# A Mamba block with expert feed-forward on one core: another order for ScalarE, TensorE and VectorE within a chunk, and another home for the convolution's sums

## The reference, cut to what matters

```
h    = x @ W.T + b + 2 * (x @ A[adapter]) @ B[adapter]             # cond, per batch adapter
u, g = split(h @ W_in.T)                                           # 2048 channels each
u    = silu(conv4(u) + conv_b)                                     # causal, 4 taps per channel
dt, Bm, Cm = rmsnorm of the parts of u @ Wx.T                      # 64 + 16 + 16
delta = softplus(dt @ Wdt.T + dt_bias)
state[t] = exp(delta[t] * A) * state[t-1] + (delta[t] * u[t]) * Bm[t]   # 16 states per channel
y[t] = sum over the 16 states of state[t] * Cm[t];  y = (y + u * D) * silu(g)
x2   = x + y @ W_out.T
z    = x2 @ base_W + base_b + lora(x2);  8 experts of rank 64, the 2 best by softmax gate
out  = x2 + sum over experts of weight * (z @ A_e.T) @ B_e.T
```

## Time and profile before

| | |
|---|---|
| median of 3 timed runs | 2613.73 us (2610.88 to 2616.55) |
| profiled execution | 2611.66 us, span 2609.9 us |
| busy: PE, DVE, POOL, ACT | 2321.2, 2239.9, 2121.8, 1622.4 us |
| granted TensorE clock, mean | 0.95 |
| first scan, end of last scan | 135.7 us, 2546.5 us |

### The profile page before, as it was taken

The page is one execution under the profiler, slowest core; times in us unless marked ns, Lnnn a source line. Parts: engine busy times, 40 slices in busy tenths (PEclk is TensorE's granted clock), DMA queues, the critical chain, the costliest instruction groups (busy, mean ns, idle before and its releaser), DMA issues.

```text
span 2609.9 us, 30425 instructions
## 1 busy us (share of the span) xinstructions
PE 2321.2 (89%) x10128; PEld 1911.7 (73%) x10128; DVE 2239.9 (86%) x2084; ACT 1622.4 (62%) x3751; POOL 2121.8 (81%) x1092
## 2 busy tenths in 40 slices
PE   8977998799989999899989999899988987786968
PEld 6866675488777878688777878688777866665857
DVE  1277777589999999999999999999999999999892
ACT  1466555466667766776667766776667766775550
POOL 0087776689889998999889998999889998999770
PEclk9988998899999999899999999899999999888989
DMA  6352433434346434543336434544336333522322
GB/s 213 125 199 85 113 105 111 129 124 137 113 127 199 140 128 131 182 145 137 113 127 199 141 128 131 182 145 137 112 107 202 126 108 101 170 92 97 121 84 97
DMA packets 131511, 350.04 MB, mean 134 GB/s; under 512 B 38609, under 2 KB 43217, under 8 KB 129883
## 3 DMA queue, kind: packets, MB, share of 16 engines
q1 hardware_dynamic: 108600, 296.18, 35.1%
q10 hardware_dynamic: 22756, 51.92, 6.0%
HBM read 337.03 MB, written 11.02 MB: 133 GB/s over the span
## 4 chain that ended last, share of the span: by engine, by line
PE 55%; POOL 14%; DVE 13%; ACT 9%; issue 7%; DMA 1%; ACTq 0%; SPq 0%; POOLq 0%; DVEq 0%
PE ubank L573 9%; PE gbank L594 8%; PE late L639 8%; DVE scan L1196 7%; POOL st L1396 6%; POOL st L1404 6%; ACT scan L1038 4%; PE gbank L603 4%; PE small L555 3%; PE late L674 3%; DVE st L1208 3%; PE late L555 3%; PE scan L573 2%; PE small L755 2%; PE late L613 2%
## 5 line engine op out<-in xcount | busy, mean ns | idle before, releaser
L1196 DVE TENSOR_TENSOR_SCAN scan<-scan,st 128x1024 f32<-128x1024 f32 x512 | 1153.4, 2285 | 192.5 <-ACT scan L1038 171.8
L1396 POOL TENSOR_TENSOR st<-w_sb,bc 128x1024 f32<-128x1024 f32 x512 | 1196.9, 2358 | 77.7 <-PE gbank L603 49.8
L1038 ACT ACTIVATE scan<-delta,A_sb 128x255 f32<-128x255 f32 x2048 | 846.5, 459 | 0.0
L1404 POOL TENSOR_TENSOR st<-st 128x1024 f32<-128x1024 f32 x256 | 603.0, 2356 | 214.9 <-DVE st L1208 204.9
L594 PE MATMUL gbank<-h,wt 128*128 128x256 f32 x2048 | 488.3, 394 | 20.1 <-DVE yg L1222 19.4
L594 PEld LDWEIGHTS gbank<-h,wt 128*128 128x128 f32 x2048 | 402.7, 198 | 93.2 <-DVE yg L1222 27.1
L1208 DVE TENSOR_TENSOR st<-scan,bc 128x1024 f32<-128x1024 f32 x384 | 455.2, 1213 | 0.0
L573 PE MATMUL ubank<-h,wt 128*128 128x256 f32 x1712 | 419.2, 401 | 0.0
L639 PE MATMUL late<-yg,wt 128*128 128x256 f32 x1792 | 401.2, 382 | 0.0
L1035 ACT ACTIVATE scan<-iota 128x4 f32<-128x4 f32 x512 | 86.6, 169 | 501.3 <-DVE st L1208 455.9
L573 PEld LDWEIGHTS ubank<-h,wt 128*128 128x128 f32 x1712 | 348.1, 204 | 58.2 <-issue 3.6
(11 more groups left out here) (193 smaller groups left out, 2445.7 us busy)
## 6 DMA issues: line engine op xcount, KB each, us to landing
wt<-in_W_in SPq DMA_DIRECT2D x256, 512.0 KB, 3.7
wt<-in_W_out SPq DMA_DIRECT2D x128, 512.0 KB, 3.3
wt<-in_cond_W SPq DMA_DIRECT2D x64, 512.0 KB, 3.6
bc<-bc_rows ACTq DMA_DIRECT2D x64, 512.0 KB, 6.5
wt<-G_tiles SPq DMA_DIRECT2D x32, 512.0 KB, 3.7
wt<-in_ffn_B SPq DMA_DIRECT2D x32, 512.0 KB, 3.4
xb<-in_x SPq DMA_DIRECT2D x8, 1024.0 KB, 6.2
x<-in_x ACTq DMA_DIRECT2D x28, 256.0 KB, 3.6
```

What stands on the lines that cost most here:

```text
L1038: last = fn(t[:, k, 1:T], delta[:, c, 1:T], ACT.Exp, scale=A_sb[:, col:col + 1])
L1196: v_.tensor_tensor_scan(Tps[q % 2][:, :], Tps[q % 2][:, :], x_, 0.0, ALU.mult, ALU.add).then_inc(scan_done, 1)
L1396: tt(st[:, n % ST_RING, :, :], w_sb[:, i % 2:i % 2 + 1, :].to_broadcast([P, NQ, T]), bc[:, 0, q * NQ:(q + 1) * NQ, :], ALU.mult).then_inc( ...
L1404: tt(st[:, n % ST_RING, :, :], st[:, n % ST_RING, :, :], st[:, (n - 1) % ST_RING, :, :], ALU.add).then_inc(add_done, 1)
```

## The change

ScalarE: decay 2 comes first in the slot (behind the evacuations), then the u evacuation of the chunk that TensorE made in the slot before, the evacuation of the half job, decay 3, silu of the gate, silu of u, the table load, and decay 0 and 1 of the next chunk. Softplus moves up to the slot's start.

TensorE: the gate chunk goes to the right half of `ubank`, the u chunk stays in the left half. Jobs get three lanes: late (bank `late`), small (bank `small`) and half (right half of `gbank`), dealt out anew over the slots, with single-block jobs `Bs`; xp and the first dt job become an end job behind the gate chunk. The order is late, small, state sum, half, u, gate, end job, and the parts of the last batch's W_out. u and gate wait for silu of the gate and for the u evacuation.

VectorE: y_sum and y_gate come behind the last product; y_sum also waits for the half job. The taps come between `add_first` and scan 2, one slot later. They add up in a new SBUF tile `cv`, into which ScalarE writes the fourth tap; only the 16 chunks of the prologue keep PSUM. The softmax's second half is spread over one slot in six steps.

G: gate and expert columns lie together (`GT_all`), and each of the 8 steps is a matmul with 264 and one with 256 columns instead of one with 8 and one with 512. The bias row is made in four column groups of TensorE and stored as four rows.

```diff
 def u_evac(v):
-    fn(o[:, T:2 * T], o[:, 0:T], ACT.Identity, bias=cb[:, c:c + 1], scale=cw[:, c, TAPS - 1:TAPS]).then_inc(u_ev, 1)
+    fn(cv_home(v), o[:, 0:T], ACT.Identity, bias=cb[:, c:c + 1], scale=cw[:, c, TAPS - 1:TAPS]).then_inc(u_ev, 1)
+def cv_home(v):
+    return quarter(v % 4)[:, T:2 * T] if v < NC else cv[:, v % 2, :]
 def conv_tap(v, k):
-    cv = u_home(v)[:, T:2 * T]
-    v_.scalar_tensor_tensor(cv, up[:, e, k:k + T], cw[:, c, k:k + 1], cv, ALU.mult, ALU.add)
+    v_.scalar_tensor_tensor(cv_home(v), up[:, e, k:k + T], cw[:, c, k:k + 1], cv_home(v), ALU.mult, ALU.add)
@@ TensorE, a slot
-    sum_states(i - 1); run(first_job(i), i); u_chunk(us[0]); out_part; run(late_job(i), i)
-    u_chunk(us[1]); run(last_job(i), i); gate_chunk(i + 1)
+    run(late_job(i), i); run(small_job(i), i); sum_states(i - 1); run(half_job(i), i)
+    ubank_free(i)                        # q_done(i + 1), u_ev of the slot before
+    u_chunk(v) for v in us; gate_chunk(i + 1); run(end_job(i), i); out_part
@@ ScalarE, a slot
-    evac(late, last of i - 1); u_silu(i - 1); wait gate_mm; silu of gate; exp table
-    decay(i, 2); decay(i, 3); evac dt, wT; u_evac(i); softplus; decay(i + 1, 0); decay(i + 1, 1)
+    evac(late, small, end of i - 1); softplus; decay(i, 2); wait gate_mm; u_evac(i - 1); evac(half of i - 1)
+    decay(i, 3); silu of gate; u_silu(i - 1); exp table; decay(i + 1, 0); decay(i + 1, 1)
@@ VectorE, a slot
-    scan 0; evac; scan 1; evac; mul 0; mul 1; add_first; scan 2; scan 3; y_sum; y_gate; mul 2; mul 3; taps(i)
+    scan 0; evac; scan 1; evac; mul 0; mul 1; add_first; taps(i - 1); scan 2; scan 3; mul 2; mul 3; y_sum; y_gate
@@ a g job
-    mm(gbank[:, T + k * E:T + (k + 1) * E], wt[kk], GTg[:, kk, :]); mm(o[:, :], wt[kk], GTx(kk))
+    mm(o1, wt[kk], GTx(kk)[:, 0:GX]); mm(o2, wt[kk], GTx(kk)[:, GX:])      # GX = 264
...
```

More of the change, by code:

```diff
@@ L163, in job_tiles @@
         return [("B", b, k)]
+    if kind == "Bs":
+        return [("Bs", b, k)]
     if kind == "g":
@@ L173, in slot_tiles @@
     tiles = []
-    us = u_chunks(i)
-    if first_job(i):
-        tiles += job_tiles(first_job(i))
+    for job in (late_job(i), small_job(i), half_job(i)):
+        if job:
+            tiles += job_tiles(job)
     if i == 0:
         tiles += [("cond", 1, m) for m in range(4, KH)]
-    if us:
-        tiles += [("u", us[0], 0)]
+    tiles += [("u", v, 0) for v in u_chunks(i)]
+    if i + 1 < CHUNKS:
+        tiles += [("gate", i + 1, 0)]
+    if end_job(i):
+        tiles += job_tiles(end_job(i))
     if part_job(i):
@@ L440, in softplus_of @@
         def softplus_of(i):
[L442 to L448, removed]
+            return [job[1:] for job in slot_jobs(i - 1) if job[0] == "dt"] if i >= 1 else []
         @block.sync
@@ L675, in expert_in, with expert_one, transformed @@
                 return mm(o, b2g[:, m * P:(m + 1) * P], la2[:, :], start=False, stop=True)
+            def expert_one(f, m, o):
+                n = TILE_NO[("Bs", f, m)]
+                pe.wait_ge(*loaded(n))
+                for k in range(EK):
+                    last = mm(o, wt[:, n % W_RING, k, :], hw[:, k, :], start=(k == 0), stop=(k == EK - 1))
+                return last
+            def transformed(rows, o1, o2):
+                for kk in range(KH):
+                    mm(o1, rows(kk), GTx(kk)[:, 0:GX], start=(kk == 0), stop=(kk == KH - 1))
+                    last = mm(o2, rows(kk), GTx(kk)[:, GX:], start=(kk == 0), stop=(kk == KH - 1))
+                return last
             def weights_t(o):
@@ L757, in run @@
+                    transformed(lambda kk: wt[:, n % W_RING, kk, :], o[:, 0:GX],
+                                late[:, 0:T] if k < KH - 1 else gbank[:, T:2 * T]).then_inc(inc, 1)
                 elif kind == "b2":
                     pe.wait_ge(b2_ld, 16 * B)
-                    rows = [b2_all[:, kk, :, :].rearrange("p b r -> p (b r)") for kk in range(KH)]
+                    pe.wait_ge(yg_done, i - 1)
+                    transformed(lambda kk: b2_all[:, kk, :, :].rearrange("p b r -> p (b r)"), o[:, 0:GX],
+                                gbank[:, T:2 * T]).then_inc(inc, 1)
+                else:
+                    pe.wait_ge(yg_done, i - 1)
@@ L771, in run @@
+                        last = mm(gbank[g:g + 1, T:2 * T], base_bias[:, kk:kk + 1], GTx(kk)[:, GX:],
+                                  start=(kk < GR), stop=(kk >= GR))
                     last.then_inc(inc, 1)
@@ L1330, in _ @@
                 mul(i, 1)
+                if weigh:
+                    soft_max_step(b - 1, 3)
                 add_first(i)
-                if b and c == 9:
-                    soft_max_in(b - 1)
+                if weigh:
+                    soft_max_step(b - 1, 4)
+                if i:
+                    for v in u_chunks(i - 1):
+                        for k in range(TAPS - 1):
+                            conv_tap(v, k)
+                if weigh:
+                    soft_max_step(b - 1, 5)
@@ L1365, in _ @@
             soft_max_in(LAST)
-            soft_max_out(LAST)
+            for n in range(6):
+                soft_max_step(LAST, n)
             for m in range(EK):
```

566 lines of the change are left out of this document (293 added, 273 removed).

## The result

The changed kernel took 2802.57 us (median of four runs, 2801.43 to 2807.97) against 2613.16 for the kernel before on the same chip: 1.073 times the time, 95% interval 1.0709 to 1.0746. It is 7% slower. The forecast was 2914 with a range of 2570 to 3010, from case A, in which the taps wait for GpSimd. The profiled run took 2807.97.

A forecast was written before the change was run, and what follows sets the result against it. No single bound at first (VectorE's own work about 279 us a batch); with waiting taps VectorE bounds. Batches 2 to 5 +220, 1 +39, 6 +51, 7 -8, 0 even: 2611.7 + 302 = 2914 us, range 2570 to 3010.

The forecast's parts named there:

- case A: Taps with two SBUF inputs each wait for the running GpSimd instruction; 2914 us, own range 2740 to 3010, chance 0.57.
- the CAST's rows: VectorE CAST with operands in SBUF: median 1.67 us, seven of eight waited for GpSimd; taken as nearest evidence for taps.
- the taps' wait per batch: VectorE's three taps a slot waiting for GpSimd, summed over the slots: 66 us a batch.
- its gain of 50: Batch 0, stage by stage, comes to 309 us without tap waits, a gain of 50; tap waits eat it.
- The 3.6 of y sum: y_sum, waiting for the half job, stalls about 1.2 us in each of slots 6 to 8, 3.6 a batch.
- the 7 of x_proj: x_proj behind u and gate in slot 12 stalls slot 13 by 4 to 6 us; with late silu 7 a batch.
- Case C: Taps don't wait; the state sum freed from silu decides, mainly in batch 0: 2539 us, chance 0.24.
- Case B: Only the first of three taps waits, 15.6 us a batch: 2609 us, about no change, chance 0.19.
- The 0.2 lost at the first tap: First tap can start at 8.45 but VectorE is there at 8.25: 0.2 us lost a slot, 3 a batch.
- decay first: ScalarE's decay 2 ahead of the u evacuation: could gain nothing in a 17.1 us slot.
- Y behind the last product: y sum and y gate moved to cover decay 0: 0.7 to 0.8 us a slot gained, in batch 7 only.
- The short products: 16 short TensorE instructions go from each of eight g jobs, 1.75 us each; only batch 0 sees it.

The follow-up runs named there:

- experiment 1: Changed kernel, but taps from chunk 16 on read u in PSUM, so they have one SBUF input; 2532.00 us, 0.969 of the kernel before.
- experiment 4: Changed kernel, but only the first of three taps has two SBUF inputs, its sum going to PSUM; 2622.80 us, 1.003 of the kernel before.
- experiment 5: 15 of x_proj's 16 products moved ahead of TensorE's silu wait in slot 12: on experiment 1's kernel 2505.29 us, on the changed kernel 2801.88 us.
- experiment 6: On experiment 1's kernel: y sum and y gate back ahead of the last two products, 2627.89 us; separately, decay 2 back behind the evacuations, 2520.31 us.
- experiment 7: Experiment 1's kernel with 16 short products of 8 columns again in each g job and the b2 job; 2566.20 us, 0.982 of the kernel before.
- experiment 2: Kernel before, with only the convolution sum cv moved from PSUM to SBUF from chunk 16 on; 2949.04 us, 1.129 of the kernel before.

## Why the prediction was right, and what it mis-sized

- **Right in sign and mechanism: case A.** The taps wait for the GpSimd instruction that runs, and the two take turns, as said. What makes them wait is the second SBUF input (experiments 1 and 4), as in the rule that the prediction cites; its other ground, the CAST's rows, was luck, as the last section shows. The mean, 1447 ns, is just under the 1.5 to 2.5 forecast.
- **The term that was too large is the taps' wait per batch.** I had 66 us; batch 2 has 50.8, batch 1 50.8, batches 3 to 5 46.7 to 49.5, batch 0 39.7 (50 as 37 + 13), batch 6 36.2 (51). The rest of the sum held: 278.9 + 3.8 + 50.8 = 333.5, and batch 2 took 333.8 (forecast 348.7). Batch 0 took 344.8, where its gain of 50 was to be eaten whole, batch 1 334.8 for 351. Of the 111 us between forecast and result 14 lie in batch 0, 16 in batch 1, 15 to 19 in each of batches 2 to 5, and 14 in batch 6. By slot of batch 2 I was too high above all where I let a tap meet a GpSimd product that in truth still waited for the state sum: slot 1 (4.3, measured 1.7) and 8 (2.5, 1.0), where neither the second nor the third tap waits, and 9 (5.9, 3.0) and 14 (6, 2.7), where the second doesn't. The state sum ends at 10 to 14 us of those slots, behind the late and small jobs, and not at 5 to 8.7. Slots 0, 3, 12 and 15 came within 1 (5.6, 4.3, 5.9, 6.1). Over the whole kernel 80 of the 112 first taps wait, 72 of the second and 55 of the third.
- **What vanishes in A vanished.** The 3.6 of y sum and the 7 of x_proj were dropped from A; experiment 5 shows 0.7 us for x_proj there, against 27 without the waits, and slot 13 of batch 2 has no gap above 0.21 us in VectorE, as A said.
- **Case C was right in its sum, in part because errors cancelled.** Without waits 2539 was forecast, and 2532.0 measured. Batch 0 gained 44 where 50 was forecast and batch 7 5 for 8, but batches 2 to 5 gained 3 to 4 each where nothing was forecast. By stage (measured, forecast): 60.2 and 59.6, 56.2 and 55.5, 118.7 and 115, 79.6 and 79, slot 0 of batch 1 21.6 and 21.5. Batch 2: 290.6 and 293.3. The stall in slot 13 was forecast at 4 to 6 and is 5.4. Y sum's stalls were put too high, at 1.2 each in slots 6 to 8: 0.4 and 1.0 in slots 7 and 8.
- **Case B fell.** The second and third taps do wait, 127 of 224 times.
- **Slot terms.** The 0.2 lost at the first tap is there (17.4 for 17.1), and gone with the evacuations first. That decay first gains nothing in a 17.1 slot held: it costs. Y behind the last product I counted only in batch 7; with the taps gone from that place it carries 0.8 in every slot, as experiment 6 shows. The sum had y there, so it is not off by that.
- **The short products** were under-counted: 12 us forecast for seven jobs, some 17 by experiment 7.
- **Batch 7** was to gain 8 and gained 3.8. In its slots 3 to 7 a scan waits 1.5 us for GpSimd, in the changed kernel and in experiment 1's.

"SBUF — State Buffer" of the Trainium skill, Who interferes with whom, was the rule that spoke against this change, and what was tried of it on the taps holds: with two SBUF inputs a wait for the end of the GpSimd instruction (experiments 2 and 4), with one none (experiment 1). The prediction's wording, that one SBUF input never waits, is too wide, as the CAST shows below.

## What to carry to other kernels

Before an operand of a VectorE instruction moves from PSUM to SBUF, count its SBUF inputs: with a second one the taps here waited for whatever GpSimd instruction was running, and the profile booked that wait as VectorE's busy time. The sign is a mean that has grown, with ends 0.28 us after GpSimd's. A cheap cure is to read one input where TensorE left it, here u in PSUM with shorter column ranges for the padding. Split a change of order and a change of operands into two kernels: here the first was worth 81 us and the second cost 271.

## What the runs showed of the hardware that I had not expected

- The loser waits for one instruction, not for a queue: with taps and GpSimd products back to back they alternate, 2.45 to 2.46 us a tap, for as long as both have work. A tap that starts 0.07 us or more ahead of the GpSimd instruction wins (47 cases), and then that one takes up to 2.63 us instead of 2.35. Five taps that started only 0.01 to 0.03 ahead lost, and took 2.65 to 2.66.
- The CAST, the nearest row of the prediction, was right for the taps by luck. It has one SBUF input, and so has the new tap of experiment 1, which never waits beside the same GpSimd. Yet the CAST still waits in experiment 1's kernel; it is short there only because it starts when little of the GpSimd instruction is left:

```profile
L1329 DVE CAST tixf<-tix x8: 154/250/355, 656.3 to 2504.9; 128x16 f32<-128x16 uint32 x8
...
946.07 2.36 POOL L1473 TENSOR_TENSOR st<-st 128x1024 f32<-128x1024 f32 x1
948.21 0.25 DVE L1329 CAST tixf<-tix 128x16 f32<-128x16 uint32 x1
```

  GpSimd ends at 948.43, the CAST at 948.46. Each CAST that starts with more than 0.2 us of a GpSimd instruction left ends 0.03 us after it: seven in the kernel before, two in the changed one, six in experiment 1's. So what makes a CAST wait is something else than a second input, and it was not tried. The same section of the Trainium skill lets a cast contend by another way than its inputs, through a mode of VectorE that takes both ports; no run here shows that.
- A wait of 50 us a batch on the bounding engine hid a fault of 6 us a batch on another so fully that removing it moved the time by 0.03%.
